# Loading pairs of chunks instead of single chunks in the second pass of a normalise, quantise and 1x1-convolve kernel

## What is computed

```
def _gn(v, G=32, eps=1e-5): ...            # mean and variance over 2 channels and all pixels of an image
def _act_quant(x):
    xc = jnp.clip(x, -8.0, 8.0)
    s = jnp.maximum(jnp.max(jnp.abs(xc)), EPS) / QMAX
    x_int = jnp.clip(jnp.round(xc / s), -QMAX, QMAX)
    ...
def _weight_quant(w):
    s = jnp.maximum(jnp.mean(jnp.abs(w), axis=(1, 2, 3), keepdims=True), EPS)
    w_q = jnp.clip(jnp.round(w / s), -1.0, 1.0)
    ...
x = x + conv1x1(_act_quant(_gn(x)), _weight_quant(weight))
```

## Time and profile before

| | |
|---|---|
| median of 3 runs | 1857.91 us (1857.57 to 1858.64) |
| the profiled execution's own time | 1858.08 us |
| its span, first to last instruction | 1856.3 us |
| moved | 524.32 MB read, 268.44 MB written, 427 GB/s over the span |
| busy: TensorE, VectorE, ScalarE, GpSimd | 57%, 72%, 59%, 24% |
| chain that ended last | DMA 66%, VectorE 16%, the rest below 7% each |

### The profile page before, as it was taken

The page is one execution under the profiler, slowest core; times in us unless marked ns, Lnnn a source line. Parts: engine busy times, 40 slices in busy tenths (PEclk is TensorE's granted clock), DMA queues, the critical chain, the costliest instruction groups (busy, mean ns, idle before and its releaser), DMA issues.

```text
span 1856.3 us, 10200 instructions
## 1 busy us (share of the span) xinstructions
PE 1057.3 (57%) x2222; PEld 314.2 (17%) x2239; DVE 1337.8 (72%) x707; ACT 1096.5 (59%) x797; POOL 451.3 (24%) x380
## 2 busy tenths in 40 slices
PE   0999999999999756433343334333433343334332
PEld 0333333333333211100000000000000000000000
DVE  4899999999999999755565556655655565556554
ACT  0999999999999777534344434443444344434442
POOL 0777777777777500000000000000000000000000
PEclk9999999999999955555555555555555555555555
DMA  9999999999999999999999999999999999999998
GB/s 407 429 428 428 429 429 427 428 429 429 429 429 427 428 416 430 431 429 431 431 430 432 431 430 431 432 430 432 431 430 433 430 431 431 430 431 432 430 431 352
DMA packets 54892, 792.90 MB, mean 427 GB/s; under 512 B 6241, under 2 KB 6241, under 8 KB 6241
## 3 DMA queue, kind: packets, MB, share of 16 engines
q1 hardware_dynamic: 36000, 524.30, 66.3%
q10 hardware_dynamic: 18880, 268.48, 33.8%
HBM read 524.32 MB, written 268.44 MB: 427 GB/s over the span
## 4 chain that ended last, share of the span: by engine, by line
DMA 66%; DVE 16%; issue 6%; ACT 4%; POOL 3%; another core or an unknown queue 2%; PE 2%; SPq 0%; DVEq 0%; ACTq 0%; POOLq 0%
DMA out_dram<-ring 36%; DMA ring<-in_x_dram 31%; DVE square_maxs L493 6%; DVE ring L597 6%; POOL levels L298 3%; ACT levels L428 2%; PE product L640 1%; DVE first_sq_maxs L503 1%; DVE levels L591 1%; ACT ring L322 1%; ACT product L315 0%; PE product L636 0%; ACT product L341 0%; SPq L223 0%
## 5 line engine op out<-in xcount | busy, mean ns | idle before, releaser
L674 PE MATMUL product<-levels,w_lhsT 128*128 128x512 bf16 x1007 | 478.4, 626 | 705.2 <-DVE levels L591 701.9
L428 ACT ACTIVATE levels<-ring,tile_affine 128x2048 int16<-128x2048 f32 x240 | 490.2, 2087 | 586.6 <-DMA ring<-in_x_dram 573.9
L597 DVE SCALAR_TENSOR_TENSOR ring<-product,out_scale,ring 128x2048 f32<-128x2048 f32 (+1 forms) x258 | 600.2, 2327 | 0.1
L493 DVE TENSOR_REDUCE square_maxs<-ring 128x4096 f32 (+1 forms) x119 | 524.5, 4418 | 27.7 <-ACT ring L322 23.4
L298 POOL TENSOR_TENSOR levels<-ring 128x512 f32<-128x512 f32 x360 | 448.9, 1275 | 183.1 <-DMA ring<-in_x_dram 180.4
L591 DVE TENSOR_SCALAR levels<-levels 128x2048 bf16<-128x2048 int16 (+1 forms) x258 | 176.1, 683 | 439.7 <-ACT levels L428 437.6
L322 ACT ACTIVATE ring<-ring,group_stats 128x4096 f32<-128x4096 f32 x119 | 441.5, 3710 | 12.5
L640 PE MATMUL product<-levels,neg_mean 128*128 128x512 f32 x720 | 364.8, 617 | 12.2
L674 PEld LDWEIGHTS product<-levels,w_lhsT 128*128 128x128 bf16 x1024 | 110.3, 130 | 1072.5 <-DVE levels L591 818.3
L636 PE MATMUL product<-ring,neg_mean 128*128 128x512 f32 x480 | 236.7, 616 | 3.3 <-DMA ring<-in_x_dram 3.2
L640 PEld LDWEIGHTS product<-levels,neg_mean 128*128 128x128 f32 x720 | 118.7, 189 | 239.3 <-POOL levels L298 205.6
(11 more groups left out here) (83 smaller groups left out, 51.9 us busy)
## 6 DMA issues: line engine op xcount, KB each, us to landing
ring<-in_x_dram SPq DMA_DIRECT2D x250, 2048.0 KB, 16.2
out_dram<-ring ACTq DMA_DIRECT2D x126, 2048.0 KB, 43.5
out_dram<-ring ACTq DMA_DIRECT2D x4, 1024.0 KB, 7.2
levels<-in_L_conv_weight_dram ACTq DMA_DIRECT2D x2, 16.0 KB, 8.9
```

The costliest lines, as they stand in the source:

```text
L428: nc.scalar.activation(levels[:, h, :], halves[:, 2 * s + h, :], ACT.Identity, bias=tile_affine[:, a, 1, :], scale=tile_affine[:, a, 0, :] ...
L493: nc.vector.tensor_reduce(square_maxs[:, bass.ds(k + 1, 1)], ring[:, slot1(REST + g), :], AX_X, ALU.max).then_inc(maxed, 1)
L597: nc.vector.scalar_tensor_tensor(part, product[:, h, at], out_scale[:, :], part, ALU.mult, ALU.add).then_inc(combined, 1)
L674: mm = pe.matmul(product[:, h, n * BANK:(n + 1) * BANK], w_lhsT[:, :], ints[:, h, n * BANK:(n + 1) * BANK], start=True, stop=True)
```

## The change

The loads of images 2 to 15 are issued as pairs of neighbouring chunks: c = 0 and 1, 2 and 3, 4 and 5, 6 and 7. A pair is 128 partitions x 8192 float32, 32 KB of consecutive memory a partition, and fills two neighbouring slots. It waits for the stores of both slots and raises the semaphore of the first one alone. The last two chunks of image 15 stay single loads. All stores stay as they were. So that a pair lies in neighbouring slots, `EARLY` is now 14 for 15: chunk 14 goes to slot 0 for slot 8, and every later chunk one slot further. On ScalarE the odd chunks of images 2 to 15 have no wait for a load, but for the very last; the last image is written out behind the loop of the others.

```diff
-    EARLY = min(SLOTS + KEPT, 2 * TC - 1)
+    EARLY = 2 * TC - 2
...
+    x_pairs = flat.rearrange("(t p d e) -> t d p e", p=P, d=TC // 2, e=2 * COLS)
...
+        pairs = ring[:, :, :].rearrange("p (d s) f -> p d (s f)", s=2)
...
+            def load_pair(t, c):
+                s = slot2(t, c)
+                sp.wait_ge(stored[s], 16 * (uses2(t, c) - 1))
+                sp.wait_ge(stored[s + 1], 16 * (uses2(t, c + 1) - 1))
+                sp.dma_start(pairs[:, s // 2, :], x_pairs[t, c // 2]).then_inc(loaded[s], 16)
+
+            for m in range(KEPT, 2 * TC):
+                load2(m // TC, m % TC)
+            with sp.Fori(2, TILES - 1) as t:
+                for c in range(0, TC, 2):
+                    load_pair(t, c)
+            for c in range(0, TC - 2, 2):
+                load_pair(TILES - 1, c)
+            for c in range(TC - 2, TC):
+                s = slot2(TILES - 1, c)
+                sp.wait_ge(stored[s], 16 * (uses2(TILES - 1, c) - 1))
+                sp.dma_start(ring[:, s, :], x_rows[TILES - 1, c]).then_inc(loaded[s], 16)
...
-                    act.wait_ge(loaded[s], 16 * uses2(t, c))
+                    if c % 2 == 0 or (isinstance(t, int) and t == 1):
+                        act.wait_ge(loaded[s], 16 * uses2(t, c))
+                    elif isinstance(t, int) and c == TC - 1:
+                        act.wait_ge(loaded[s], 16 * uses2(2, c))
...
-            with act.Fori(2, TILES) as t:
+            with act.Fori(2, TILES - 1) as t:
                 row_tile(t)
+            row_tile(TILES - 1)
```

More of the change, by code:

```diff
@@ L63, in preact_quant_conv_kernel @@
     assert PRE + TURNS * TURN == N1 and KEPT_PARTS * PIECE == KEPT * COLS and len(FIRST_PIECES) + TURNS - 1 == KEPT_PARTS
-    assert TC < EARLY <= 2 * TC and TC == RING2 and REST <= RING1
+    assert SLOTS <= EARLY and TC == RING2 and REST <= RING1
+    assert (RING1 + EARLY - SLOTS) == RING2 and KEPT % 2 == 0
     flat = x.rearrange("b c h w -> (b c h w)")
@@ L241, in load2 @@
                 m = t * TC + c
-                if isinstance(t, int) and m < SLOTS:
+                if m < SLOTS:
                     sp.wait_ge(maxed, USES - SLOTS + m + 1)
-                elif isinstance(t, int) and m < EARLY:
+                elif m < EARLY:
                     sp.wait_ge(kept_stored[m - SLOTS], 32 if m - SLOTS < HALVED else 16)
@@ L248, in load2 @@
                 sp.dma_start(ring[:, s, :], x_rows[t, c]).then_inc(loaded[s], 16)
[L250 to L256, removed]
+            def load_pair(t, c):
[14 more added lines that the diff above has]
+                sp.dma_start(ring[:, s, :], x_rows[TILES - 1, c]).then_inc(loaded[s], 16)
             for c in range(KEPT):
                 sp.wait_ge(kept_stored[c], 32 if c < HALVED else 16)
-            for s in range(RING1 + EARLY - SLOTS):
-                last = max(m for m in range(KEPT, CHUNKS) if slot2(m // TC, m % TC) == s)
-                sp.wait_ge(stored[s], 16 * uses2(last // TC, last % TC))
+            for c in range(TC):
+                sp.wait_ge(stored[slot2(2, c)], 16 * uses2(TILES - 1, c))
         @block.gpsimd
@@ L382, in store @@
                 s = slot2(t, c)
+                act.wait_ge(combined, EXTRA + t * (2 * TC) + 2 * (c + 1))
                 done = kept_stored[c] if isinstance(t, int) and t == 0 and c < KEPT else stored[s]
-                act.wait_ge(combined, EXTRA + t * (2 * TC) + 2 * (c + 1))
                 act.dma_start(out_rows[t, c], ring[:, s, :]).then_inc(done, 16)
```

## The result

The change makes the kernel **slower: 1920.63 us** (median of 4, 1909.18 to 1922.38) against 1857.74 us for the kernel before in the same comparison: **ratio 1.0326, interval 1.0305 to 1.0347**. The forecast was 1856.8 us, with a range up to 1863.5. What came is the slower rival's case, at 62.9 us where it gave 8.3.

What follows compares the result with a forecast made beforehand. The prediction took DMA bytes to bound the kernel throughout. Its terms, -1.9 + 0.5 + 0.3 = -1.1 us, took 1857.9 to 1856.8 us; whole range 1852.5 to 1863.5, small gain or none at chance 0.60.

Steps and rivals of the forecast that it cites:

- slower rival: Quantising pass: each pair load starts on an empty load queue, 428 GB/s all through, 1866.2 us; chance 0.20.
- What bounds the kernel: Whole kernel: DMA bytes from beginning to end, with the slowest DMA engine, some 7 us behind, setting the span.
- (a): Pair loads: 55 DMAs in place of 110 halve rows and completions; -1.9 us.
- (b): Quantising pass: long load rows get two thirds of the bytes, then stores run alone, never dry; cost zero.
- Evidence used against that rival: Transition: the load at 710.8 us also began on an empty queue, yet 712 to 724 us ran at 431 GB/s.
- (c): Transition: chunk 14's load waits for a later store, so engines may idle; +0.5 us, range 0 to 2.6.
- (d): ScalarE's unrolled last image: one or two more program fetches, counting on the engine that ends last; +0.3 us, range 0 to 1.5.
- (e): Waits taken from ScalarE's odd chunks, double waits on SP, single loads at the end: zero.
- 428 or less from 800 to 1800: Quantising pass: this rate in GB/s would show the forecast wrong for the slower rival's reason.
- A DMA share below 1 in the steady part would refute (b): Steady part of the quantising pass: sign in the profile that was to disprove the zero cost of turns.

Runs made afterwards that it cites:

- e4: The changed kernel with the stores of images 2 to 15, but for the last two chunks, also paired (32 KB rows): 1855.22 us.
- e17: The kernel before, with loads issued two together once the load before them has landed: 1875.55 us.
- e16: The kernel before, with loads issued four together once the load before them has landed: 1869.25 us.
- e7: The changed kernel with single loads, each behind its own slot's store; slot map and unrolled last image stay: 1856.49 us.
- e1: The changed kernel with each pair as two 2 MB loads of 16 KB rows, issued together: 1857.49 us.
- e2: The changed kernel with each pair one 4 MB DMA of 16 KB rows, chunks k and k + 4 of an image: 1856.39 us.
- e3: The changed kernel with the odd chunk's store issued before the next pair is waited for: 1922.73 us.
- e6: The changed kernel with all twelve slots used in the quantising pass instead of eight: 1911.21 us.
- e8: The changed kernel with single 16 KB-row loads issued two by two, and stores paired with 32 KB rows: 1878.05 us.
- e5: The kernel before, with each store split into two DMAs of 128 rows of 8 KB: 1883.64 us.
- e11: e4 with single stores in all of the last image: 1855.6 us.
- e12: e4 with single stores in all of the last image and all twelve slots in use: 1878.66 us.
- e14: The kernel before, with each load of images 2 to 15 issued only when the load before it has landed: 1947.13 us.

## Why the prediction was wrong, point by point

- *What bounds the kernel*: right, DMA from end to end. The reading, that one engine is behind the others and sets the end, was right too, and I left it in the tail where it belongs in every period: a slot is free when the slowest engine has done its share.
- *(a) Pair loads, -1.9 us*: the packet count of 28080 was exact. The saving in the row is real but tiny: 1213 against 2 x 611 ns is 9 ns for 32 KB, and e4's 432 GB/s against 431 is all that it can bring. The changed kernel shows none of it.
- ***(b) Turns between the two queues, zero*: this is the step that failed.** "Cost zero, hidden as long as stores are queued", and "The queue does not run dry". The turns were right, the cover was not. I counted the queued stores by their time to landing, which is that of the last engine. In the changed kernel fifteen engines come to have their stores done some 23 us before it, and from 1300 to 1500 us half of all load rows have no store beside them (595 of 1175, before 2 of 2620): on the fifteen the store queue did run dry, and the start of a pair is bare. On the last engine stores stay queued, as the runs of s show, and its load rows are stretched even so. While the engines were close together (800 to 900 us) a 32 KB load row was 13 ns over its 1213, 0.1 us a pair; from 1300 us on it is 151 ns over, 1.2 us a pair. Issue to issue it is +1.24 us a pair, 68 us. Pairs landed after 20.0 us, not 15, since the last engine begins 4 to 6 us after the pair's issue; my reading for that case, that loads and stores would then share by bytes, was false as well.
- *The slower rival*: the right place, the start of a pair on an empty load queue, with the wrong row for its price. I took 428 GB/s from stretches in which a load begins anew (0.14 us a pair), and had beside it the row of 326 GB/s, a start with no store beside it, 1.2 us lost. 55 x 1.2 = 66 us would have been within 4 us of the result. It should have been the upper bound of (b), and the range should have reached toward it. That the price of one start agrees is partly luck: only about a third of the extra time stands in first rows behind stores, and e17 and e16 paid 0.3 to 0.4 us.
- *Evidence used against that rival*: "712 to 724 ran at 431" behind a load that began on an empty queue. With the other slot map the same place ran at 403 and 404. One undisturbed window was too little to set against it. (e7 has no pairs, so that place says nothing of their price either.)
- *(c) one slot fewer, and (d) program text, +0.8 us*: together with the slot map they cost nothing (e7, -1.6 us, interval on both sides of zero), though the windows of (c) lost 1.7 us of rate. *(e)*: zero, as said (e1 and e2 keep the double waits and are within 0.1%).
- *The falsifiers*: "428 or less from 800 to 1800" came, with 406 from 900 on. "A DMA share below 1 in the steady part would refute (b)" was a poor one. The share is 0.99 to 1.00: a stretched packet counts as busy.

The Trainium skill (DMA: Bandwidth & Descriptors, Queues, rings and completion order) says that each engine goes round-robin between its queue rows, a packet at a time. The chains agree that it takes turns, but not on the size of one: the page gives a packet as 9 to 17 descriptors, and here the engine switches after every row. Longer rows on one queue therefore get it more bytes in a turn. Its advice to make one transfer as large as possible (SBUF — State Buffer, The DMA setup-cost knee) isn't borne out here: 4 MB for 2 MB gave 0.9994 with even rows (e2) and 1.0326 with uneven ones.

**Shown**: the unequal row lengths do it and nothing else in the edit (e1, e2, e7, e3, e4); the time is lost in stretched load rows (the shares, the chains); with it one engine falls 23 us behind, and the store queue runs dry on the others; more slots help little (e6). **Argued only**: that the long first rows of the fifteen are latency that no store covers (by the times since the issue). **Open**: why the rows of the last engine are stretched although it has stores, and so which came first, its lag or the dry queues; why load rows are long where stores begin again, which makes e17, e16 and e8 slow; what makes e5 slow; and why e4, e11 and e12 have two groups of runs.

## What to carry to other kernels

When loads and stores share the DMA engines and these are the bound, give both queues rows of the same length and keep at least two loads in flight; a time to landing is that of the slowest engine and doesn't tell whether the others have work queued; the size of a DMA matters far less (4 MB or 2 MB made no difference here). Judge such a stage by GB/s and by each queue's share per MB, never by the DMA's busy share. When a change can make a queue run empty once a period, take the worst start that the trace shows, times the periods, as the upper bound of the range.

## What the runs showed of the hardware

- A stretched packet counts as busy: a share of 0.99 to 1.00 at 400 to 409 GB/s.
- A 32 KB row is one packet and one turn, 1213 ns against 611 for 16 KB, in both directions.
- One engine of sixteen can fall behind the others: its stores land 23 us after theirs in the changed kernel, 55 us in e6, where it ends 28 us after them. The slots only choose between that tail and a lower rate all along.
- In the changed kernel only load rows stretch: of 2536 store rows, 1300 to 1500 us, none is over 618 ns. Elsewhere store rows stretch a little too: mean 618 ns in e14 and 1229 ns for 1213 in e8. In the slower group of e11 they stretch more than the loads (mean 1256 against 1220 ns).
- With 32 KB rows in both directions the same kernel has two groups of times, some 15 to 25 us apart (e11, e12). I have no explanation.
